# Moving the two products of latent values to the steps around the gathered x of a decoder-layer kernel

## The reference, cut to what matters

```python
ckv = _rms(x @ w_ckv, g_kvnorm)
v1 = (ckv @ w_dv).reshape(B, T, N_HEAD, V_HEAD)          # the latent values
scores = (x @ w_imp)[..., 0]
_, idx = jax.lax.top_k(scores, KEEP); idx = jnp.sort(idx, axis=1)
sel = jnp.take_along_axis(x, idx[:, :, None], axis=1)    # the gathered x
ks = (sel @ w_selk).reshape(B, KEEP, N_HEAD, NOPE + ROPE_D)
vs = (sel @ w_selv).reshape(B, KEEP, N_HEAD, V_HEAD)
ks = jnp.concatenate([ks[..., :NOPE], _rope(ks[..., NOPE:], cos, sin)], axis=-1)
a1 = _attn(q, k1, v1, causal=True)
a2 = _attn(q, ks, vs, causal=False)
a3 = _attn(q, kw, vw, causal=True)
out = g[:, 0] * a1 + g[:, 1] * a2 + g[:, 2] * a3
```

## Time and profile before

| what | us |
|---|---|
| median of 3 runs | 1756.48 (1752.28 to 1768.41) |
| time of the profiled execution | 1749.06 |
| its span, first to last instruction | 1747.0 |
| mean granted PE clock in it, as a share of full speed | 0.983 |

### The profile page before, as it was taken

How to read it: one execution, slowest core, us unless ns; L and a number is a source line. 1 busy time by engine, 2 the same in 40 slices (tenths; PEclk the granted TensorE clock), 3 DMA queues, 4 the chain that set the end, 5 groups by cost and what they waited for, 6 DMA issues and landing times.

```text
span 1747.0 us, 33531 instructions
## 1 busy us (share of the span) xinstructions
PE 1674.7 (96%) x11320; PEld 1356.4 (78%) x11320; DVE 1153.9 (66%) x3826; ACT 844.5 (48%) x2760; POOL 1037.1 (59%) x1451
## 2 busy tenths in 40 slices
PE   6799999999999999999999889999999999999998
PEld 5576675776776766757757569999999999999997
DVE  4467767875776677677767478565656575657557
ACT  1475857846937758568569452222222222222221
POOL 2465656745846656557458385665756575658553
PEclk9899999998999999999999899999999999999999
DMA  7203003012012030030120110101010101010001
GB/s 216 62 2 75 24 14 85 2 43 56 2 48 51 2 75 24 14 85 2 31 63 2 50 49 25 49 1 49 1 49 1 49 1 49 1 49 1 1 1 49
DMA packets 52458, 63.52 MB, mean 36 GB/s; under 512 B 12288, under 2 KB 40448, under 8 KB 52160
## 3 DMA queue, kind: packets, MB, share of 16 engines
q1 hardware_dynamic: 52288, 61.38, 12.6%
HBM read 29.89 MB, written 2.10 MB: 18 GB/s over the span
## 4 chain that ended last, share of the span: by engine, by line
PE 44%; DVE 2%; ACT 2%; issue 1%; POOL 1%; POOLq 0%; DVEq 0%; ACTq 0%
PE ps_Y L2223 20%; PE ps_H L2223 19%; PE ps_S L1437 2%; ACT pr L881 1%; PE ps_O L1437 1%; DVE h_hi L2186 1%; PE ps_T L1658 0%; ACT pr L935 0%; PE ps_X L1437 0%; PE ps_T L1776 0%; POOL pr L723 0%; DVE x L2147 0%; DVE st L2132 0%; DVE x_lo L1410 0%; POOL w_lo L730 0%
## 5 line engine op out<-in xcount | busy, mean ns | idle before, releaser
L2011 POOL TENSOR_TENSOR h_lo<-h_sb,h_hi 128x512 fp32r<-128x512 f32 x256 | 363.3, 1447 | 109.0 <-DVE h_hi L2186 109.0
L2057 ACT ACTIVATE h_sb<-ps_H,b_sb 128x512 f32<-128x512 f32 x256 | 176.7, 690 | 506.5 <-PE ps_H L2223 479.9
L688 POOL TENSOR_TENSOR pr<-pr,rden 128x128 f32<-128x128 f32 (+2 forms) x768 | 307.1, 435 | 113.5 <-DVE rden L1229 113.4
L881 ACT ACTIVATE pr<-sm,nmx 128x128 f32<-128x128 f32 (+2 forms) x768 | 311.6, 412 | 32.7 <-DVE nmx L1240 32.4
L2186 DVE CAST h_hi<-h_sb 128x512 fp32r<-128x512 f32 x256 | 239.7, 953 | 130.0 <-ACT h_sb L2057 129.9
L2223 PE MATMUL ps_Y<-w_hi,h_hi 128*128 128x256 f32 x1024 | 286.7, 280 | 0.0
L2223 PE MATMUL ps_Y<-w_hi,h_lo 128*128 128x256 f32 x1024 | 286.7, 280 | 0.0
L2223 PE MATMUL ps_Y<-w_lo,h_hi 128*128 128x256 f32 x1024 | 286.5, 280 | 0.0
L723 POOL TENSOR_TENSOR pr<-pr,rden 128x256 f32<-128x256 f32 x256 | 151.4, 613 | 130.4 <-DVE rden L1229 130.4
L1240 DVE CUSTOM_DVE_ANT_0 sm<-ps_S,cmask 128x128 f32<-128x128 f32 (+2 forms) x768 | 193.0, 308 | 51.2 <-PE ps_S L1437 29.7
L2223 PE MATMUL ps_H<-x_hi,w_hi 128*128 128x512 f32 x512 | 200.4, 391 | 0.0
(11 more groups left out here) (240 smaller groups left out, 3084.2 us busy)
## 6 DMA issues: line engine op xcount, KB each, us to landing
qT_sb<-rot SPq DMA_DIRECT2D x256, 64.0 KB, 2.0
w_raw<-in_W SPq DMA_DIRECT2D x16, 1024.0 KB, 6.3
kT_sb<-rot SPq DMA_DIRECT2D x192, 64.0 KB, 2.0
xin<-in_x SPq DMA_DIRECT2D x8, 256.0 KB, 2.7
cin<-in_ctx SPq DMA_DIRECT2D x8, 256.0 KB, 2.7
w_kw<-in_wink SPq DMA_DIRECT2D x2, 768.0 KB, 7.8
w_ks<-in_selk SPq DMA_DIRECT2D x2, 768.0 KB, 10.3
out<-x SPq DMA_DIRECT2D x3, 512.0 KB, 2.9
```

What stands on the lines that cost most here:

```text
L688: last = pool.tensor_tensor(p_, p_, rden[:, h % 2, n:n + 1].to_broadcast([P, width]), ALU.mult)
L881: last = act.activation(pr[:, h % PR_SLOTS, a:a + width], sm[:, h % 2, a:a + width], ACT.Exp, bias=nmx[:, h % 2, n:n + 1], scale=-1.0, acc ...
L2011: pool.tensor_tensor(h_lo[:, s % 2, ht, :], h_sb[:, ht % 4, :], h_hi[:, s % 2, ht, :].bitcast(F32), ALU.subtract).then_inc(lo_sb.sem, 1)
L2057: ins = act.activation(h_sb[:, ht % 4, :], pst[plan.bank(f)][:, :], ACT.Relu, bias=b1[:, 2 * i + s // NCH, ht:ht + 1])
```

## The change

The two products of latent values move on PE from h = 14 and 15 to the steps h = 9 and h = 11, which were empty. ACT's copies of them move to the same steps, h = 9 and h = 11. In the list of bank fills ("v1", 0) now stands behind `pos` and ("v1", 1) behind `xsel`, so that the banks are: `pos` S2, ("v1", 0) S3, `xsel` S2, ("v1", 1) S3, ("ks", "ab") S2, ("ks", "nv") S3. No instruction of work is added or taken away, and the number of front steps stays the same. On ACT the copy of the first transposed selected keys stays in h = 15, on PE `turn_selected` too.

```diff
--- before.py
+++ after.py
@@ -198,7 +198,7 @@
             ("kw", 1, "a"), ("kw", 1, "b"), ("kw", 1, "n"), ("vw", 0), ("vw", 1),
             ("q", 0, "a"), ("q", 0, "b"), ("q", 0, "n"), ("q", 0, "c"),
             ("q", 1, "a"), ("q", 1, "b"), ("q", 1, "n"), ("q", 1, "c"),
-            "pos", "xsel", ("ks", "ab"), ("ks", "nv"), ("v1", 0), ("v1", 1))):
+            "pos", ("v1", 0), "xsel", ("v1", 1), ("ks", "ab"), ("ks", "nv"))):
         plan.add(name, f"S{2 + n % 2}", ahead=True)
     for n, name in enumerate(("latT", ("ksT", 0), ("ksT", 1))):
         plan.add(name, ("T1", "X")[n % 2], ahead=True)
@@ -843,19 +843,19 @@
                 yield
                 yield
 
-                yield
-                yield
+                values_out("v1", 0, v1, gate[:, 0:1])
+                yield
+                yield
+
+                values_out("v1", 1, v1, gate[:, 0:1])
                 yield
                 yield
 
                 nope(4)
                 evacuate(i, ("ks", "nv"), vs[:, :], ps(("ks", "nv"))[KEEP:2 * KEEP, :], gate[KEEP:2 * KEEP, 1:2])
                 yield
-
-                values_out("v1", 0, v1, gate[:, 0:1])
-                yield
-
-                values_out("v1", 1, v1, gate[:, 0:1])
+                yield
+
                 evacuate(i, ("ksT", 0), kT[:, 0:8, 0:KEEP],
                          ps(("ksT", 0))[0:QK, :].rearrange("p (h t) -> p h t", h=8))
 
@@ -1595,6 +1595,7 @@
                 mm(ps("pos")[:, 1:2], upper[:, :], sel[:, 1:2], False, True).then_inc(plan.full_sem("pos"), 1)
                 yield
 
+                latent_values(0)
                 yield
 
                 pe.wait_ge(pick_sb.sem, pick_sb.at(i, 1))
@@ -1605,6 +1606,8 @@
                                   pick[:, t, :], t == 0, t == NT - 1)
                 last.then_inc(plan.full_sem("xsel"), 1)
                 yield
+
+                latent_values(1)
                 yield
 
                 if i == 0:
@@ -1615,11 +1618,8 @@
 
                 selected(("ks", "nv"), [w_ks[:, c, 0, :] for c in range(NC)], [w_vs[:, c, :] for c in range(NC)])
                 yield
-
-                latent_values(0)
-                yield
-
-                latent_values(1)
+                yield
+
                 turn_selected()
 
             def scores(i, h):
```

## The result

| | before | after |
|---|---|---|
| median of 4 runs, us | 1754.4 (1748.6 to 1768.4) | 1739.0 (1735.0 to 1739.3) |
| profiled execution, us | 1749.06 | 1735.02 |
| its span, us | 1747.0 | 1733.0 |
| mean granted PE clock in it | 0.983 | 0.989 |

The ratio is 0.9894, with a 95% interval of 0.9862 to 0.9926. The change saves about 15 us, 1.1%. I had forecast about 3 us less and a range that ends at 1744, so the prediction was wrong: the gain is real and lies outside it.

A forecast was written before the change was run, and what follows sets the result against it. PE, busy 96% of the span, was taken as the bound. 1749.06 us plus 1.75 for seven longer turns less 4.7 for the clock gave 1746.1; adding 7.42 to reach the median gave 1753.5, range 1744 to 1766.

The forecast's parts named there:

- Step 1: ("v1", 0) at h = 9 fills PE's 0.92 us wait for ACT's copy and delays PE by 0.10 us.
- Step 2: xsel goes into bank S2, which is free whenever pick is; no cost.
- Step 3: ("v1", 1) at h = 11, where PE had no wait, costs 1.05 us; everything behind shifts by 1.15 us in all.
- Step 4: ("v1", 0) gone from h = 14: PE waits 0.35 us for POOL ahead of the transposes of head 12.
- Step 5: ("v1", 1) gone from h = 15: turn_selected waits 0.86 us for POOL's second sum and starts 0.25 us later.
- Step 6: End of the chain: DVE's key copy and the scores of head 0 come 0.25 us later, lengthening each turn by that.
- the third rival: Keys are ready when PE reaches turn_selected, so the moved products save PE time: 1745.1 us, chance 0.11.
- The clock: Two drops in h = 9 go (-6.50 us), drops at the keys rise from two to three (+1.77): -4.7 us.
- the second rival: The clock falls at the selected keys, ahead of head 0's scores, in each turn: 1760.6 us, up to 1783.3; chance 0.14.

The follow-up runs named there:

- v11_h10: The changed kernel with PE's product ("v1", 1) moved from h = 11 to right behind xsel in h = 10: median 1740.7 us, 0.9928 of before.
- keys_first: The changed kernel with POOL's sums of the selected keys in h = 12 and turn_selected with its copies in h = 14: median 1724.9 us, 0.9839 of before.
- v11_h13: The changed kernel with ("v1", 1) moved to the end of h = 13, in bank X, and its ACT copy to h = 14: 1741.0 us.
- v10_h7: The changed kernel with ("v1", 0) and its ACT copy moved from h = 9 to h = 7: median 1745.8 us, 0.9945 of before.
- only_v10: The changed kernel with ("v1", 1) back in h = 15, ("v1", 0) staying in h = 9: median 1738.6 us, 0.9908 of before.
- only_v11: The changed kernel with ("v1", 0) back in h = 14, ("v1", 1) staying in h = 11: median 1745.2 us, 0.9953 of before.
- keys_early: The changed kernel with the selected keys' products, rotation and transposes one cross step earlier on all engines: median 1761.9 us, 1.0038 of before.

## Why the prediction was wrong

The direction was right and the size was not. By its steps:

- *Step 1, ("v1", 0) at h = 9.* Right. I took a delay of 0.10 us and it was 0.00: the scores start at the same place in the turn. ACT's copy went into its idle time.
- *Step 2, `xsel` in bank S2.* Right, no cost.
- *Step 3, ("v1", 1) at h = 11.* This is the step that failed, and with it the sentence that it rests on, that a moved product "costs PE the same wherever it stands". I took 1.05 us, the distance between two starts in h = 14, with bounds of 1.05 and 1.25 on the shift. It costs 0.0 there. In its old places its neighbours were values and transposes, of 128 rows, and in h = 15 the 64-row transposes behind it, and it overlapped with none of them. In the new one it is followed by products of 32 rows in other rows of the array. The distance between two starts is what a group costs only beside the neighbours that it was measured with. The row that I read, `32*128` in front of the shape, said how many rows it needs; I did not ask which rows, or who comes next. v11_h10 measures the step as I had it: the scores of heads 12 and 13 come 1.19 us later than in the changed kernel (I had 1.15 in all), and a turn is 119.30 us against my 119.21.
- *Step 4, a new wait ahead of the transposes of head 12.* There is one of 0.51 instead of 0.35 us, and it is not POOL's. POOL's product ended at 299.40 + 1.18 = 300.58. What PE waits for is bank S0, which DVE empties with the reduction from 300.28 to 300.70, as the bracket at 300.86 says. I had looked for the data of this step and not for its bank. This error is one of its own: v11_h10, with step 3 at its full price, has the same 0.51 us behind DVE.
- *Step 5, `turn_selected` bound by POOL's second sum.* Right in the mechanism. The bracket names nobody, but in the changed kernel, in v11_h10 and in keys_first PE starts 0.10 to 0.11 us behind the end of the sum. The sum ends at 301.77 + 1.26 = 303.03, which is 303.96 in the stamps of before, as if nothing had moved. The new wait is 0.65 us (0.86 forecast), and the start is 0.83 us earlier instead of 0.25 later: 0.83 of the slack of 0.94 that I had found was collected, since the sum did not move by 1.15; the other 0.11 lies between the sum's end and PE's start.
- *Step 6, the scores of head 0.* 0.86 us earlier; the wait for the key copy is 0.40 instead of 0.50. My lower bound for a turn was -0.95, by the mechanism of the third rival, "POOL is not the bound". The turn came close to that bound by another way: POOL is the bound, and its input was not late.
- *The clock.* The sign and the place were right. Both drops in h = 9 went, as I forecast, but of the drops at the keys there was one instead of three. So the term is -8.3 and not -4.7. With the 0.92 us wait open the clock fell in h = 9 and 10 in 9 of 21 turns, and with it filled in none. That agrees with the rule of the Trainium skill that I had named (page "TensorE: Matmul & The Clock Gate", section "A second HAM failure mode: psum-queue depth-cycling"), that frequent short idle times make the clock oscillate. Where I expected it to bite, at 0.65 and 0.40 us around the transposes, the clock fell in one turn of seven, so the second rival and its "each turn" did not come. That the wait ahead of `turn_selected` brings drops at the keys is not shown either: they came in 9 of the 35 turns that have a wait of 0.65 us or more there (changed, v11_h10, v11_h13, v10_h7, keys_first) and in 3 of the 21 that do not (before, only_v10, only_v11), too few to tell apart.

In numbers, for the profiled execution: 7 x (0.25 + 0.85) = 7.7 us too much for the quiet turns and 3.6 too much for the clock are 11.3, and the forecast of 1746.1 missed 1735.0 by 11.1. The forecast of the median, 1753.5, missed by 14.5: the other 3.4 are in what I added from the profiled execution to the median, 7.4 where it is 4.0 in the changed kernel. I also set the chances badly: 0.93 for "within 1%", a limit that the result passed by little (1.1%), rested on one price that I had not bounded from below. Had I put 0 as the lower bound of step 3, the range would have reached 7 x 1.05 us further, to about 1737, and held the result.

## What to carry to other kernels

The price of a small product is not a property of the product. The one of 32 rows here cost its full time between products of all rows, its full time ahead of transposes of 64 other rows, and nothing ahead of products of 32 other rows; so when a product is moved, look how many rows of the array its new neighbours use, and which. Where PE is nearly always busy, a wait of under 1 us can cost more by the clock than by itself: filling it gave no time in a quiet turn and 6 us over the kernel. And an engine that ends a chain with much idle time of its own (POOL here) can hold PE by the order of its queue; another order on POOL and PE (keys_first) shortened a quiet turn by 1.1 us, where the whole change had given 0.85.

## What the runs showed of the hardware that I had not expected

- A product of 32 rows (96 to 127) and eight score products in rows 0 to 63 take 1.07 us together, where either alone takes 1.05 or 1.06. Beside heads in rows 64 to 127 only the four in rows 64 to 95 overlap with it, and the whole takes 1.91. Ahead of 64-row transposes in rows 0 to 63 nothing overlaps: 1.05 us.
- The granted clock fell behind a wait of 0.92 us in 9 of 21 turns, always to 1.2 GHz, and in none of 35 turns in which that wait was filled. A slow stretch cost its turn about half of its length: 1.5 us at 541.7 us in the changed kernel, where it lasted 3.4, and 3.4 us at 172.2 us in v10_h7, where it lasted 6.8. A wait of 2.2 us in each turn (keys_early) left a mean clock of 0.976 to 0.978, the lowest of all kernels here.
